# GpSimd's step of the attention in a one-core attention and expert block: the order of its operations

## The reference

```python
def _L0_xattn_ref(emb, context, Wq, Wk, Wv, Wu, bu, qn_w, qn_b, kn_w, kn_b):
    ...
    q = _layernorm(q, qn_w, qn_b)
    k = _layernorm(k, kn_w, kn_b)
    scale = 1.0 / jnp.sqrt(jnp.asarray(KQ_DIM, emb.dtype))
    attn = jnp.einsum('bhqd,bhkd->bhqk', q, k) * scale
    attn = jax.nn.softmax(attn, axis=-1)
    out = jnp.einsum('bhqk,bhkd->bhqd', attn, v)
    out = out.transpose(0, 2, 1, 3).reshape(B, SQ, N_HEADS * KQ_DIM)
    return out @ Wu.T + bu
...
    logits = x @ Wg
    probs = jax.nn.softmax(logits, axis=-1)
    vals, idx = jax.lax.top_k(probs, TOP_K)
    ...
    out = jnp.einsum('te,teh->th', cw, y)
    shared = jax.nn.silu(x @ Ws1 + bs1) @ Ws2 + bs2
    out = out + SHARED_SCALE * shared
```

## Time and profile before

| what | value |
|---|---|
| median of 3 timed runs | 632.81 us |
| lowest and highest of them | 631.47, 633.86 us |
| span of the profiled execution, first to last instruction | 671.8 us |
| busy share of the span: PE, DVE, ACT, POOL | 87%, 68%, 67%, 54% |
| attention, about 20 to 424 us: PE and POOL busy between 42 and 209 us | 164.6 and 97.6 of 167 us |
| the same between 213 and 404 us, where scatters run | 178.3 and 132.0 of 191 us |

### The profile page before, as it was taken

How to read it: one execution, slowest core, us unless ns; L and a number is a source line. 1 busy time by engine, 2 the same in 40 slices (tenths; PEclk the granted TensorE clock), 3 DMA queues, 4 the chain that set the end, 5 groups by cost and what they waited for, 6 DMA issues and landing times.

```text
span 671.8 us, 21158 instructions
## 1 busy us (share of the span) xinstructions
PE 586.6 (87%) x7642; PEld 517.3 (77%) x7642; DVE 456.0 (68%) x997; ACT 453.3 (67%) x986; POOL 361.4 (54%) x706
## 2 busy tenths in 40 slices
PE   3889999999999999999999987868979988989930
PEld 1578888888888887877887865766979988989930
DVE  4688889898998888887888874464244534444418
ACT  3688899999897887887887863532525444545425
POOL 2545656565666677677677564554105535545530
PEclk9899999999999999999999999978989989999985
DMA  7900100001001001002000000123102212212228
GB/s 242 282 2 3 34 18 29 24 3 49 4 17 43 26 14 47 25 12 64 11 14 16 10 14 21 34 92 100 41 1 77 76 59 71 73 65 77 73 87 316
DMA packets 22583, 38.01 MB, mean 57 GB/s; under 512 B 5233, under 2 KB 13041, under 8 KB 22353
## 3 DMA queue, kind: packets, MB, share of 16 engines
q1 hardware_dynamic: 17648, 27.27, 12.8%
q0 software_dynamic: 4544, 9.38, 3.9%
q10 hardware_dynamic: 288, 0.00, 0.0%
HBM read 23.17 MB, written 13.47 MB: 55 GB/s over the span
## 4 chain that ended last, share of the span: by engine, by line
PE 74%; DVE 8%; issue 7%; DMA 3%; POOL 2%; ACT 2%; another core or an unknown queue 1%; SPq 0%; ACTq 0%; DVEq 0%; POOLq 0%
PE ps L1317 9%; PE ps L1091 7%; PE ps L1147 7%; PE ps L1059 6%; PE ps L1117 6%; PE ps L1061 5%; PE ps L1060 5%; PE ps L1100 4%; PE ps L1219 4%; PE ps L1132 4%; PE ps L1303 3%; PE ps L1305 3%; PE ps L1304 3%; DMA rows_all<-results 1%; DVE wide L754 1%
## 5 line engine op out<-in xcount | busy, mean ns | idle before, releaser
L670 POOL DMA_INDIRECT results<-spo,xs_ix x78 | 75.2, 965 | 100.9 <-DVE spo L1033 85.9
L522 ACT ACTIVATE qk_T<-ps,b_cols 128x256 f32<-128x256 f32 x156 | 61.8, 475 | 75.7 <-PE ps L1305 74.3
L396 ACT ACTIVATE qk_T<-ps,lnw 128x512 f32<-128x512 f32 x128 | 96.8, 787 | 6.0 <-PE ps L1091 5.4
L1059 PE MATMUL ps<-w_hi,xc_hi 128*128 128x512 f32 x192 | 88.3, 460 | 7.9 <-DVE wide L754 3.7
L754 DVE TENSOR_TENSOR wide<-ps,rstd 128x512 f32<-128x512 f32 x128 | 87.2, 681 | 3.9 <-POOL rstd L612 3.9
L747 DVE TENSOR_REDUCE ss<-wide 128x16 f32<-128x1024 f32 x64 | 77.9, 1218 | 15.5 <-ACT wide L372 13.9
L636 POOL DMA_INDIRECT routed<-rows_all,slot x64 | 64.4, 1006 | 29.9 <-issue 16.0
L1091 PE MATMUL ps<-ident,wide 128*128 128x128 f32 x512 | 78.4, 278 | 2.1 <-DVE wide L754 1.0
L372 ACT ACTIVATE wide<-ps 128x512 f32<-128x512 f32 x128 | 76.1, 596 | 3.2 <-PE ps L1061 3.2
L1061 PE MATMUL ps<-w_hi,xc_lo 128*128 128x512 f32 x192 | 77.2, 402 | 0.0
L1317 PE MATMUL ps<-w_sb,qk_T 128*128 x624 | 76.9, 277 | 0.0
(11 more groups left out here) (169 smaller groups left out, 1323.4 us busy)
## 6 DMA issues: line engine op xcount, KB each, us to landing
v_sb<-routed SPq DMA_DIRECT2D x39, 130.0 KB
xc_in<-in_x SPq DMA_DIRECT2D x8, 256.0 KB, 2.9
xc_in<-in_ctx SPq DMA_DIRECT2D x8, 256.0 KB, 4.5
w_raw<-in_L_ffn_W SPq DMA_DIRECT2D x8, 256.0 KB, 2.5
wide<-results SPq DMA_DIRECT2D x4, 512.0 KB, 5.1
rows_all<-results SPq DMA_DIRECT2D x4, 512.0 KB, 8.0
out_x<-x_res SPq DMA_DIRECT2D x8, 256.0 KB, 4.1
x_res<-in_x SPq DMA_DIRECT2D x1, 1792.0 KB, 8.5
```

What stands on the lines that cost most here:

```text
L396: nc.scalar.activation(qk_T[:, n, 4 * j:4 * j + 4, :].rearrange("p a n -> p (a n)"), ps[6 + j][:, :], ACT.Identity, bias=lnw[:, 2 * n + 1: ...
L670: gp_.indirect_dma_start(out=results[:, :], out_offset=bass.IndirectOffsetOnAxis(ap=xs_ix[:, b4, a:a + 1], axis=0), in_=yb[:, b4, a, :], i ...
L1059: nc.tensor.matmul(out_bank, xc_hi[:, t % XD, src, :], w_hi[:, w, cols[j]], start=True, stop=False)
```

## The change

Only the order of the calls in POOL's `step(s)` changes. The other engines' lists stay as they are.

```diff
             def step(s):
-                scatter(s - SCATTER_LAG)
-                variance(1, s)
-                newton_step(1, s)
                 output_bias(s - 2)
                 token_eps(s + 1)
                 expert_weights(s - 1)
                 low_part(s + 3)
                 second_rstd(s - 3)
+                variance(1, s)
+                newton_step(1, s)
+                scatter(s - SCATTER_LAG)
                 variance(0, s + 1)
                 newton_step(0, s + 1)
                 normalise_rows(s - 1)
```

## The result

| what | value |
|---|---|
| changed kernel, median of 4 runs | 643.16 us (642.04 to 646.88) |
| kernel before, median of 4 runs | 632.18 us (631.47 to 633.86) |
| ratio, with its 95% interval | 1.0182 (1.0158 to 1.0206) |

A forecast was written before the change was run, and what follows sets the result against it. It took PE alone to bound steps without scatters (11.14 us) and the loop over `prob` those with them. 632.8 + 1.5 (with scatters) + 0.5 (without) = 634.8 us; own range 631 to 639, full range 613 to 643.

The forecast's parts named there:

- Rival 2: DVE's L788 held 0.3 to 0.5 us, statistics and key `rstd` late, PE's cover exceeded: 8 us, 641 us; chance 0.19.
- the sentence on steps without scatters: Late L754 and `prob`, 0.2 us, mostly covered by PE's spare time after `prob`: 0.5 us in all.
- DVE waits 0 to 0.15 us, and this is on the loop that binds: Steps with scatters: L754 waits for the key `rstd`, 0.1 us over 15 steps, 1.5 us.
- the hold of L788: DVE's L788 blocked at the port shared with POOL's small operations: 0 to 0.3 us, no cost.
- PE's cover of 0.3: PE takes `prob` 0.41 us after its end, a hand-over needs about 0.1; the 0.3 left absorbs lateness.
- the stalls of the scores: Idle gaps in PE's scores beside scatters, 1.21 us a step, 19.4 us; taken as absent from timed runs.
- rival 3: The scores' stalls are real in timed runs, so 19.4 us go: 615.4 us; chance 0.26.
- the 39: Profiled span of 671.8 us against the timed median of 632.8: 39 us with no place in a timed run.
- scatters behind the key norms: POOL's two scatters run from about T + 4.4 to T + 6.8, with 0.8 us slack before the query norms.
- the end of the stage: The last scatters shift 2.5 us later, taken up by POOL's 5.41 us wait for the last batch's slots: 0 us.
- T + 2.6 for the statistics: Rival 2's deciding sign: it holds once DVE's statistics (L739) end after T + 2.6.

The follow-up runs named there:

- the version without the hold: Changed kernel with `expert_weights` and `low_part` also moved behind the scatters, `second_rstd` still ahead of the key norms: 636.01 us, ratio 1.0035.
- the second trace: The unchanged kernel before, run and profiled once more with no edit: 631.92 us, with a span of 630.1 us.

## Why the prediction was wrong

The forecast was 634.8 us and the time 643.16, just outside the range. Rival 2 (641 us, chance 0.19) is what happened, up to the late key `rstd`; how that `rstd` costs time, it had wrong too.

- **The step that failed** is the sentence on steps without scatters: "PE takes `prob` only 0.41 us after its end ... The 0.3 left cover it: 0 us for most steps". I followed the late L754 to `prob` and stopped. A second one waits for the end of L754: PE's next projection, which writes the bank that L754 reads, and it had no slack (L754's end to the projection 0.14 us before, 0.15 us where PE waits). The order of calls on PE and two rows of the trace would have shown it. For the stretch without scatters the forecast was 0.5 us, and 5.5 us were measured.
- **With scatters the path was right and the size wrong.** "DVE waits 0 to 0.15 us, and this is on the loop that binds", 1.5 us; L754 comes 0.34 us later in the mean, up to 0.85, and the measured cost is 5.4 us. In nine of these 15 steps PE takes `prob` within 0.12 us of its end. How much of the 5.4 us goes over `prob` and how much over the bank stays open.
- **The size of the lateness.** Forecast T + 4.85 without scatters; it was T + 5.16, and T + 4.85 in the version without the hold. The 0.3 us are the hold of L788, taken "0 to 0.3 and no cost". That it costs nothing by itself is right (0.9995 with the hold and `second_rstd` behind). I took it so because DVE then waits for the scores; but POOL waits for the statistics in between, which rival 2 said. Rival 2 gave the price as 0.25 us a step after "PE's cover of 0.3"; without cover it is 0.54 in the step shown. That its 8 us came near the 11 measured is in part luck: it counted 0.25 us in 31 steps, and L754 came about 0.55 us later in nine of the 15 without scatters, and by nothing to 0.85 us in the others.
- **Why the hold is there in so many steps.** Against rival 2 stood that POOL waits for `w_hi` while the port is free. That wait lets L630 start together with L788 instead: the argument counted a wait as free time and did not ask when it ends.
- **Right: the stalls of the scores.** They are in neither trace of a usual execution, and rival 3 falls. But the reasoning was weaker than its result. The two traces of the kernel before differ by 41.7 us, and only 15.6 us of these lie between the scores of tile 0 and those of tile 31. Behind them the first trace takes 270.3 us and the second 243.0, so 27 us did come from elsewhere, where the prediction "found nothing of that size". The guess that the stalls come from recording beside descriptors isn't borne out, since the second trace records the same instructions beside the same scatters. Nor do the 6 us that the prediction took off the 39 appear: the span lies 1.8 us below the timed value of the same execution. The changed kernel's span is 30.8 us below 671.8, not the 17 to 20 forecast. What drew out the first execution stays open.
- **Right: scatters behind the key norms and the end of the stage**, 0 us each within the interval: the version with only `second_rstd` put back has both and takes 0.9995. At the end POOL waits 6.32 us for the last `mv`, and the rest of the queue follows it.
- **The chances.** Rival 2 depended on one number, T + 2.6 for the statistics, and I had the parts for it: L630 or L586 beside L788 at T + 1.4. By these it deserved more than 0.19.

## What to carry to other kernels

Follow a late operand to everything that its reader releases, and to everything behind the reader on its own list: an instruction that reads a PSUM bank (the memory that TensorE writes its results to) frees it as well as making data, and the wait of the next writer may be the tight one. An operation that fills an idle stretch ahead of an urgent chain is free only if nothing in it waits for another engine; if it does, that engine's lateness, here DVE's held L788, becomes the chain's. And before a stall in a trace is priced, the span is set against the timed runs: here 39 us of difference meant that the trace was of a drawn-out execution. The search for the missing time has to cover the whole span, and here most of it lay outside the stage that was read.

## What the hardware showed

- Two engines at one port. The Trainium skill (SBUF — State Buffer, "Who interferes with whom") says of DVE in its two-port modes, which it says `tensor_scalar` can enter, that whoever issues first gets the shared pair for the whole instruction. The version with `expert_weights` behind agrees: L586 starts at 136.75 and ends at 137.48, and L788, which starts 0.23 us behind it, takes 0.59 us instead of 0.34. Where POOL's L630 and DVE's L788 start within 0.02 us, L788 takes 0.66 us and its follower starts 0.59 us after it. Who issued first can't be read there, and in the step with scatters L788 takes 0.68 us although L630 starts 0.08 us behind it in the profile. The next POOL instruction, L586 at 136.17, follows L630 with no gap, and L788 ended at 136.29 all the same: it was held for one instruction of POOL, not for two in a row.
- One execution of the same program spanned 671.8 us and showed up to 0.6 us of empty time in the supply of PE's small matmuls; another spanned 630.1 us, and between 42 and 418 us none of its 31 gaps ahead of L1117 was above 0.2 us. Nothing in the program differs.
